# A two-stage conditioned residual: the last store of a streaming kernel issued as 120 channels and 8 channels

## What is computed

```python
def _L0_cond_ref(x, weights, condition):
    W = weights[condition]
    return jnp.einsum('bct,bcd->bdt', x, W)

def _L1_cond_ref(x, subjects, weights, biases):
    w = weights[subjects]
    b = biases[subjects]
    out = jnp.einsum('bct,bcd->bdt', x, w)
    return out + jnp.transpose(b, (0, 2, 1))

x = x + _L0_cond_ref(x, L0_cond_weights, itok_B_0_15)
x = x + _L1_cond_ref(x, itok_B_0_31, L1_cond_weights, L1_cond_biases)
```

## Time and profile before

| | |
|---|---|
| median of the runs | 648.29 us (647.83 to 648.33) |
| the profiled execution | 646.94 us |
| its span, first to last instruction | 645.2 us |
| TensorE busy, share of the span | 79% |
| VectorE, ScalarE, GpSimd busy | 31%, 24%, 20% |
| moved by DMA | 271.71 MB, 421 GB/s over the span |
| DMA share, 60 to 600 us | 1.01, at 428 GB/s |

### The profile page before, as it was taken

One profiled execution on the slowest core, in us unless ns is written; L12 is line 12 of the kernel. 1 busy time (PEld: TensorE's weight loads), 2 busy tenths in 40 slices (PEclk: granted clock), 3 DMA queues, 4 the chain that ended last, 5 costly groups with the idle time before them and its releaser, 6 DMA issues.

```text
span 645.2 us, 5659 instructions
## 1 busy us (share of the span) xinstructions
PE 511.0 (79%) x1280; PEld 236.1 (37%) x1280; DVE 201.6 (31%) x256; ACT 152.8 (24%) x136; POOL 127.9 (20%) x391
## 2 busy tenths in 40 slices
PE   1999798787987867987778889778897787888971
PEld 0444343333443333433333334333343343333430
DVE  0344333322322323323223333232333232323320
ACT  0233222222322223222222222221222222312220
POOL 2222211112112112112121121121211211112100
PEclk9999988999989999889998898998999998989997
DMA  8999999999999999999999999999999999999996
GB/s 358 411 429 425 427 428 427 426 429 427 428 428 427 428 427 427 428 428 427 428 428 427 428 428 427 428 428 428 427 428 428 427 428 428 427 428 428 427 427 258
DMA packets 35259, 271.71 MB, mean 421 GB/s; under 512 B 2225, under 2 KB 2226, under 8 KB 2226
## 3 DMA queue, kind: packets, MB, share of 16 engines
q1 hardware_dynamic: 17696, 137.37, 50.5%
q10 hardware_dynamic: 17554, 134.24, 49.2%
HBM read 137.38 MB, written 134.22 MB: 421 GB/s over the span
## 4 chain that ended last, share of the span: by engine, by line
DMA 77%; PE 18%; ACT 2%; issue 1%; SPq 0%; another core or an unknown queue 0%; ACTq 0%
DMA xt<-in_x_dram 44%; DMA out_dram<-xt 34%; PE left L143 5%; PE left L144 4%; PE right L148 4%; PE right L149 4%; ACT xt L206 2%; PE comb L134 1%; SPq L92 0%; ACTq L211 0%; SPq L86 0%; SPq L85 0%; ACTq L205 0%; ACTq L210 0%
## 5 line engine op out<-in xcount | busy, mean ns | idle before, releaser
L188 DVE TENSOR_SCALAR xt<-left,bias_b 128x1024 f32<-128x1024 f32 x128 | 164.3, 1283 | 326.6 <-PE left L144 323.7
L206 ACT ACTIVATE xt<-right,bias_b 128x1024 f32<-128x1024 f32 x128 | 142.5, 1113 | 424.1 <-PE right L149 424.0
L143 PE MATMUL left<-xt,both 128*128 128x512 f32 x256 | 144.4, 647 | 102.7 <-DMA xt<-in_x_dram 102.7
L112 POOL TENSOR_TENSOR map0T<-w0T_sb,ident 128x128 f32<-128x128 f32 x128 | 58.2, 454 | 485.5 <-issue 407.2
L144 PE MATMUL left<-xt,both 128*128 128x512 f32 x256 | 142.4, 640 | 0.0
L148 PE MATMUL right<-xt,both 128*128 128x512 f32 x256 | 137.5, 620 | 4.8 <-ACT xt L206 4.8
L149 PE MATMUL right<-xt,both 128*128 128x512 f32 x256 | 131.3, 595 | 0.0
L143 PEld LDWEIGHTS left<-xt,both 128*128 128x128 f32 x256 | 39.7, 196 | 113.9 <-DMA xt<-in_x_dram 100.8
L148 PEld LDWEIGHTS right<-xt,both 128*128 128x128 f32 x256 | 51.5, 204 | 76.1 <-issue 49.0
L134 PEld LDWEIGHTS comb<-map,map0T 128*128 128x128 f32 x256 | 48.9, 192 | 74.1 <-issue 60.6
L144 PEld LDWEIGHTS left<-xt,both 128*128 128x128 f32 x256 | 51.9, 203 | 65.9 <-issue 65.9
(11 more groups left out here) (2 smaller groups left out, 0.1 us busy)
## 6 DMA issues: line engine op xcount, KB each, us to landing
xt<-in_x_dram SPq DMA_DIRECT2D x64, 2048.0 KB, 38.2
out_dram<-xt ACTq DMA_DIRECT2D x64, 2048.0 KB, 31.5
w_sb<-in_w_dram SPq DMA_DIRECT2D x1, 2048.0 KB, 9.4
w0T_sb<-in_w0T_dram SPq DMA_DIRECT2D x1, 1024.0 KB, 4.9
cond_sb<-in_conds_dram ACTq DMA_DIRECT2D x1, 1.0 KB
bias_sb<-in_bias_dram ACTq DMA_DIRECT2D x1, 16.0 KB, 9.5
```

Of the source, the lines that this page charges most:

```text
L112: nc.gpsimd.tensor_tensor(map0T[:, s % 2, :], w0T_sb[:, bass.ds(i0, 1), :], ident[:, :], ALU.add).then_inc(map0_ready, 1)
L143: nc.tensor.matmul(left[:, 0:CHUNK], both[:, s % 2, :], xt[:, s, 0:CHUNK], start=True, stop=True)
L188: nc.vector.tensor_scalar(xt[:, s, 0:HALF], left[:, :], bias_b[:, s:s + 1], None, ALU.add).then_inc(left_out, 1)
L206: nc.scalar.activation(xt[:, s, HALF:T], right[:, :], ACT.Identity, bias=bias_b[:, s:s + 1]).then_inc(right_out, 1)
```

## The change

ScalarE's loop runs over 7 turns, and the eighth is written out after it. The loop's body becomes a function `group(turn, last)`. In the written-out turn the last store of the kernel is left out of the body and issued behind it as two transfers: channels 0 to 119 on the semaphore of the pair, and channels 120 to 127 on a new semaphore `rest_stored`, for which ScalarE waits at the very end. Loads, products, additions and all other stores are as they were.

```diff
+    MOST = 120
...
+        rest_stored = sem("rest_stored")
...
-            with act.Fori(0, TURNS) as turn:
+
+            def group(turn, last):
                 first = turn * SLOTS
                 for s in range(SLOTS):
                     b = first + s
...
                     if s % 2 == 1:
                         act.wait_ge(left_out, b + 1)
                         act.wait_ge(right_out, b + 1)
+                    if s % 2 == 1 and not (last and s == SLOTS - 1):
                         act.dma_start(out_pairs[:, bass.ds(turn * PAIRS + s // 2, 1), :, :],
                                       xt[:, s - 1:s + 1, :]).then_inc(stored[s // 2], LOAD)
+
+            with act.Fori(0, TURNS - 1) as turn:
+                group(turn, False)
+            group(TURNS - 1, True)
+
+            act.dma_start(out_pairs[0:MOST, B // 2 - 1, :, :],
+                          xt[0:MOST, SLOTS - 2:SLOTS, :]).then_inc(stored[PAIRS - 1], LOAD)
+            act.dma_start(out_pairs[MOST:C, B // 2 - 1, :, :],
+                          xt[MOST:C, SLOTS - 2:SLOTS, :]).then_inc(rest_stored, LOAD)
             for q in range(PAIRS):
                 act.wait_ge(stored[q], LOAD * TURNS)
+            act.wait_ge(rest_stored, LOAD)
```

## The result

| | before | changed |
|---|---|---|
| median of the runs | 647.83 us (646.70 to 648.33, 7 runs) | 651.05 us (649.90 to 652.42, 7 runs) |
| the profiled execution | 646.94 us | 650.66 us |
| its span | 645.2 us | 648.9 us |

The ratio is 1.0056, with a 95% interval of 1.0044 to 1.0067: slower by about 0.6%, 3.6 us by the ratio (3.2 us between the two medians), where 4.1 us of gain were forecast. The median of before is lower here than in the table ahead because more runs are in it.

What follows compares the result with a forecast made beforehand. The kernel was taken as bound by DMA, with one late engine alone at the end. Relieving it, less the 8-channel store's rows, moved the end from 644.3 to about 640.2: 648.29 - 4.1 = 644.2 us, range 643.2 to 650.0.

Steps and rivals of the forecast that it cites:

- What bounds the kernel: Whole kernel: a stream of DMA transfers; at the end one late engine works alone for 4.7 us, one share behind.
- the choice of the idle engine: 120-channel store: fifteen shares of 8 channels leave one engine free, taken to be the late one.
- The term of -4.90 us: 120-channel store: the late engine gets none of its rows and ends one share earlier, 4.90 us before 644.3.
- rival 3: Last store: the late engine is one of the 15, keeps 16 rows, perhaps 2 more; 648.3 to 648.9 us; chance 0.20.
- the rate of the 15: 120-channel store: the 15 engines run side by side at full rate, as in every row of before; no loss counted.
- Rival 1: Last stores: engine pairs share one on-chip path, 2 x 0.306 us a row; 648.5 to 650.4 us; chance 0.22.
- the 2.45 us for the rest: 8-channel store: upper case, its 8 engines no faster than two; 0.61 us was taken, 2.45 kept for the range.
- the range's 650.0: Measured time: upper end of the 8-in-10 range, 643.2 to 650.0, leaving out the fullest meeting of engines.
- The second issue: ScalarE's queue at the end: issuing the 8-channel store costs nothing; 0.4 us if the cover were gone.
- the written-out turn at no cost: ScalarE's last turn: 0 to 0.1 us gain expected from less waiting and register work, counted as 0.
- Seven table loads: ScalarE: one activation table load of 8 goes, leaving 7 or so; worth nothing in time.
- Signs: Last DMA windows: no lone stretch, share 0 by about 640.2 if right; share near 1 at half the GB/s if engines meet.

Runs made afterwards that it cites:

- The whole store: Changed kernel with its last store put back as a single 128-channel transfer, ScalarE's last turn still written out: 647.88 us, ratio 1.0009 to before.
- the store by sample: Changed kernel with the last store as two transfers of 128 channels, one per sample: 647.98 us, ratio 1.0014 to before.
- the marks: Against the changed kernel: last pair's first 1,792 columns in one 128-channel store, last 256 in stores of 80, 12, then 1 to 8 channels: 647.46 us, one run.
- 112 and 16: Changed kernel with the last store cut into 112 and 16 channels in place of 120 and 8: 651.49 us, ratio 1.0072 to before.
- 7 and 1: Changed kernel with the 8 channels behind the 120 stored as 7 and 1: 651.31 us, ratio 1.0072 to before.
- 4 and 4: Changed kernel with the 8 channels behind the 120 stored as 4 and 4: 649.84 us, ratio 1.0038 to before.
- the version with the first four: Against the changed kernel: last pair's first 1,600 columns in one 128-channel store, last 448 in stores of 124 and 4 channels: 648.04 us, ratio 1.0009 to before.

## Why the prediction was wrong

**What bounds the kernel** was right. One engine is alone for 4.7 us at the end, its last share is 16 rows, and its end sets the span. The whole store, the store by sample and the marks all show the same stretch.

**The first step that failed is the choice of the idle engine.** The text took 120 channels as fifteen shares of 8, which is right (15 landing marks), and chose that the late engine is the one left out. It is among the 15 and among the 8, the fifth by the marks if the order is fixed, and the trace has its 16 rows of the 120-channel store between the marks of 642.56 and 647.46. The term of -4.90 us for its 16 rows was therefore 0, and it received two of the rest, 0.62 us. That is rival 3, which had a chance of 0.20; it was priced at 0 to 0.6 us, and measured at 0.6. The text said itself that nothing in the trace named the engine, and still gave its choice more than half the chance.
The packet counts here are those of 15 engines for 120 channels, 8 for 8, 16 for 112 and for 16, 7 for 7, 2 for the one channel of two samples and 4 for 4. That a store uses the first engines of a fixed order was assumed: the late engine had rows of the stores on 16, 15, 8 and 7 engines and none of the store on 4, which fits it, and no run tests it by itself.

**The second step that failed is the rate of the 15, whose loss the sum put at nothing.** "Engines have run side by side at full rate in every row of before" was true, and said nothing about another cut: in before every large transfer had 128 channels and, as the text took it, every engine a fixed set of them, which no trace shows. Rival 1 was right in kind: most slow rows took 0.58 to 0.645 us where it gave 2 x 0.306. Fifteen took up to 1.24 us, more than two engines in turn would need, and what met there is open. Its size for the end came out differently. It took the meeting to lengthen the last store on all engines, to 644.5 to 646.4; the other engines had their last mark at 644.23. That alone was the end of the forecast's gain. What set the end was the late engine, which was still reading its share of the store **before** when the others began the new one, and was slowed there by 3.4 us. The four kernels that cut the large store by channels give 7.6 to 8.5 us for that share (120 and 8; 112 and 16; 7 and 1; 4 and 4), and before, the whole store and the store by sample 4.9 us. The text had no term for this share.
The runs show that neighbours on chip are slow together (56 and 48 of the last 128 rows over 0.36 us), channels 4 apart are not (none in either run), and that the output's side does not matter. They show neither that four neighbours have one path, as P had it, nor which channels each engine reads in a store of 120 or of 128, and so not at which channels the late engine was met. Two terms of the prediction were the author's estimates and no run shows them: that two engines share a path at 2 x 0.306 us a row, and the 2.45 us for the rest at the rate of two engines, which is in 646.1 and 650.4. In their place the runs showed the slow rows just named, and 0.62 us for the late engine's two rows of the rest.

**The two rivals were priced one by one and happened together.** Each alone left the time near before or a little above; the sum, 3.4 + 0.6 us, lies above the range's 650.0. A range built from single rivals had no place for their sum, although nothing made one exclude the other.

**The second issue and the written-out turn at no cost** were about right: the whole store behind the written-out turn is 0.1% above before, with an interval that touches no change, and the two stores by sample are 0.14% above it. Seven table loads and no further fetch came as said.

**Signs.** The share did not fall to zero at 640.2; the lone stretch stayed, and of the share near 1 at half the GB/s, the sign of rival 1, the windows have 0.94 at 243 GB/s, nearer 0.6 than half.

## What to carry to other kernels

When a stream of DMA ends with one engine alone, find out which engine it is before giving it less: small stores of 1, 2, 3 and so on channels behind the last large one, counted by their landing marks, told its place in one run here, once the late engine was alone when it came to them. A cut by channels made rows slow in all four kernels that had one on the large store; a cut by sample, with all 128 channels in each transfer, left every row at 0.31 us and cost about 0.1%. A change in the last transfer also acts on what an engine that is behind still has to do from the one before.

## What the runs showed of the hardware

- One engine, the fifth by its marks if stores use the first engines of a fixed order, falls steadily behind and ends a whole share (16 rows, 4.7 to 4.9 us) late after 645 us. In before, the last step of the semaphore of the turn's last store lags the fifteenth by 0.4 us at 111 us and 0.0 us at 190 us, and in the turns after by 0.9, 1.8, 2.7, 3.5 and 4.4 us: 0.86 us, or 1.1%, a turn. At the end it is 4.8 us. Why, and why not from the start, is open: this was not tried.
- When engines read neighbouring channels on chip at the same time, a row of 8 KB takes longer than its 0.31 us: 56 and 48 of the last 128 rows in the two runs with sixteen such stores, none in the two with channels 4 apart on chip, whether or not they are neighbours in the output. That it is pairs of engines that meet is not shown. In the changed kernel most slow rows (87 of 121 from 634 to 641) took 0.58 to 0.645 us.
- An engine that is behind is slowed as well: its share of the store before took 7.6 to 8.5 us instead of 4.9 when the last store was cut by channels.
- A store of 8 channels holds ScalarE's queue for 0.73 to 0.83 us when sixteen follow each other (11.7 to 13.3 us in all), against 0.38 us for one of 2,048 KB.
- Not shown: whether the late engine can be relieved at all near the end. If its channels can only be read at the rate of one engine, as the slow rows of the version with the first four suggest (three of its rows took 0.45 to 0.59 us instead of 0.244), its rows would have to be moved while the kernel still runs, and not in the last transfer. That wasn't tried.
